# A four-block tower on one core: when the dense heads' pieces run in the last stage

## The chip, the cores and the metric

The kernel runs as one program on one core of a Trainium2 chip. Its time is the device time of one execution in microseconds; before the change the median of 3 runs is 13776.14 us (13771.75 to 13789.44).

## The reference, cut to what matters

The reference is a tower of four blocks over 4 sequences of 2048 tokens with 64 channels. The change touches only the last half block, a product-key memory attention with 8 heads:

```python
q = (x @ Wq).reshape(b, n, HEADS, DIM) * DIM ** (-0.5)
kv_scores, indices = _pk(x, Wq_pk, pk_keys)   # 16 of 64 x 64 keys, per token and head
ind = indices + offsets[None, None, :, None]
k = jnp.einsum('bnhk,bnhkd->bnhd', kv_scores, keys_table[ind])
v = jnp.einsum('bnhk,bnhkd->bnhd', kv_scores, values_table[ind])
sim = jnp.einsum('bihd,bjhd->bhij', q, k)
sim = jnp.where(causal, sim, neg)
attn = jax.nn.softmax(sim, axis=-1)
out = jnp.einsum('bhij,bjhd->bhid', attn, v)
return out.transpose(0, 2, 1, 3).reshape(b, n, HEADS * DIM) @ Wo
```

Each token and head picks 16 of 4096 table rows, mixes them with softmax weights into one key and one value, and then the head runs causal attention over its 2048 tokens.

## The kernel before, in words

The stage `mix_heads` works on 32 (sequence, head) pairs. 20 of them are "gathered" heads (kind `g`): GpSimd fetches the 16 rows of each token by indirect DMA (L2278), ScalarE scales them (`part_up`, L2479) and VectorE sums them (L2714). 12 are "dense" heads (kind `d`): no row is fetched; the whole table of the head lies in SBUF and is multiplied by a weight matrix that is made piece by piece. Each pair is cut into 4 quads of 512 tokens, a quad into 4 tiles of 128 tokens. So there are DQ = 48 dense quads, GQ = 80 gathered quads, and 512 tiles.

**A dense quad is 32 pieces** (one per 128 rows of the table's 4096), numbered k over all quads, 1536 in all. One piece is:
- `level` (TensorE, L2369): one bf16 matmul, 128x512, of the ranks into a PSUM bank, `DX` or the last bank of `S`;
- `lift` (ScalarE, L2521): a Relu of the bank into `V`;
- `cross` (TensorE, L2375 three times and L2376): four bf16 matmuls into the same bank;
- `grow` (ScalarE, L2525): Exp of the bank into `W`;
- `blend` (TensorE, L2385): an f32 matmul, `values` times `W`, summed up in `acc`.

After 32 pieces VectorE scales `acc` (`store`, L2743), and ScalarE copies it out when the quad's queries are made.

**The order is written out by hand, by sub-steps** s = 0 to 536. Every engine runs the same loop over s in its own in-order queue. In sub-step s, tile n = s - 24 is attended, the 16 picks of one tile of quad s // 4 are found on VectorE, 10 copies (COPIES) of gathered rows are scaled on ScalarE, and the pieces of `pieces(s)` are run. A tile at depth i in its sequence attends over i + 1 blocks of 128 keys, in chunks of four blocks: a quad g has 1, 2, 3 or 4 chunks by g % 4. Each chunk is a `flip` (TensorE transposes of the probabilities, L2343), a `take_flip` (ScalarE, L2517) and a `mixing` (TensorE, L2353).

In a sub-step TensorE and ScalarE interleave these in turns c = 0, 1, ...; there are as many turns as the most of chunks, pieces and extras (extras make q, k, v, ranks and the like, at most 4 of them):

```python
for c in range(turns(s)):
    if c < chunks(s):
        flip(n, c)
    if c < len(todo):
        cross(todo[c])
    if c < chunks(s):
        mixing(n, c)
    for use in extras(s)[c:c + 1]:
        extra(use)
    if c + 1 < len(todo):
        onward(todo[c + 1])
```

`onward(k)` is `blend(k - 1)` and `level(k)`. ScalarE does take_flip, grow, the extra, three copies of `part_up` and the next lift in each turn; the ten copies are out after the third turn and one more. `spare` and `second` choose the bank: pieces alternate between `DX` and the last bank of `S`, except beside tiles that need that bank of `S` (depth 12 and up in this or the next tile), where all go to `DX`.

A tile begins with `scores` (L2336), which waits for the Exp of the tile before (`attend`, ScalarE, L2508), as `S` is one buffer; `attend` waits for VectorE's `peak` (L2725). VectorE's `scale` (L2734) of tile n comes after `peak` of tile n + 1 and waits for the last `mixing` of tile n.

`first_piece(s)` (in the kernel before: 1536 pieces over 512 sub-steps, 3 in each from s = 9 to 520) decides which pieces a sub-step has. `pick_order` sorts the quads by a due sub-step so that picks come before gathers and pieces; `attend_order` is the fixed order in which quads are attended. SyncE reloads each quarter of `values` when its eight tiles are blended.

Of the kernel before, what the change touches and what calls it, by code (L numbers as in the profile page):

```python
# [4 lines left out]

# [1 line left out]

# [1958 lines left out]
HEADS, KEYS, TOPK, KV = 8, 64, 16, 2 * D  # L1968
# [4 lines left out]

PERIOD, BEFORE = 20, (0, 2, 4, 5, 8, 9, 10, 12, 14, 16, 18, 19)
LAG, UNITS_FROM, PIECES_FROM = 6, 12, 9
QUAD = 4
DQ, GQ = QUAD * len(D_HEADS), QUAD * len(G_HEADS)
QUADS = DQ + GQ
STEPS = QUAD * (QUADS + LAG) + 1
TILES = KEYS * KEYS // P  # L1980
COPIES = TOPK * GQ // QUADS
# [88 lines left out]
def gather_quad(g):  # L2070

    return *G_HEADS[g // QUAD], g % QUAD


def dense_quad(d):

    return *D_HEADS[d // QUAD], d % QUAD


def first_piece(s):  # L2080

    return TILES * DQ * (s - PIECES_FROM) // (QUAD * QUADS)


def pick_order():

    def due(kind, i):
        if kind == "g":
            return UNITS_FROM + QUAD * TOPK * i / COPIES - 6
        return PIECES_FROM + QUAD * QUADS * i / DQ - 9  # L2090

    return sorted([("g", i) for i in range(GQ)] + [("d", i) for i in range(DQ)], key=lambda x: (due(*x), x[0]))


def attend_order():

    order, d = [], 0
    for g in range(GQ):
        if g % PERIOD in BEFORE:
            order.append(("d", d))  # L2100
            d += 1
        order.append(("g", g))
    return order


def mix_heads(nc, table, h, hT, ident, ones, wsim, iota, wq, wo, mask, lanes, sel, counts, push, least):

    wsim_h = wsim[:].rearrange("d (p h k) -> d h p k", p=2, h=HEADS)
    picks, attends = pick_order(), attend_order()
    kinds = [attends[n // QUAD] for n in range(QUAD * QUADS)]  # L2110
    depth = [QUAD * (kinds[n][1] % QUAD) + n % QUAD for n in range(QUAD * QUADS)]
# [16 lines left out]
    def pieces(s):  # L2128

        return list(range(max(first_piece(s), 0), max(min(first_piece(s + 1), TILES * DQ), 0)))  # L2130
# [63 lines left out]
    with Scope(nc, "l3m") as u:  # L2194
# [91 lines left out]
        def _(pe):  # L2286
# [139 lines left out]
            for s in range(STEPS):  # L2426
                n, nxt = tile_at(s), tile_at(s + 1)
                todo = pieces(s)
                if todo:
                    onward(todo[0])  # L2430
                elif pieces(s - 1):
                    blend(TILES * DQ - 1)
                if nxt is not None:
                    scores(nxt, max((k + 1 for k in second if k < first_piece(s)), default=0))
                if n is not None:
                    pe.wait_ge(expd, n + 1)
# [11 lines that stand above are left out]
# [494 lines left out]
```

## Time and profile before

| what | us |
|---|---|
| median of 3 runs | 13776.14 |
| lowest and highest run | 13771.75, 13789.44 |
| span of the profiled execution | 17300.9 |
| of it, the stage of the change (from about 5850 on) | about 11450 |

The profiled execution's own time is its span, 17300.9 us; no unprofiled time is recorded for it, and it is 25.6% over the median of the runs. PE is TensorE's matmul, PEld its weight load, DVE VectorE, ACT ScalarE, POOL GpSimd, SP SyncE. In a row of a timeline the first number is the start in us from the span's start, the second the duration in us, and in square brackets stands the idle time of that engine just before and what ended it. "remote" and "another core or an unknown queue" stand where the profile cannot name what ended an idle time.

### The profile page before, as it was taken

The page shows a single profiled execution, that of the slowest core. Times are in us where ns is not written, and L with a number is a line of the kernel's source. Part 1 is how long each engine was busy: PE and PEld are TensorE (multiplying, and loading weights), DVE is VectorE, ACT ScalarE, POOL GpSimd, SP SyncE. Part 2 cuts the span into 40 slices and gives each one's busy share as a digit, 9 for nine tenths or more (in the row PEclk, how much of TensorE's full clock was granted, in tenths as well). Part 3 has the DMA queues.
Part 4 walks back from the last instruction along what each step waited for, and adds up shares of the span by engine and source line. Part 5 has one row for each costly group of instructions (what it writes and reads, how often), then busy time and mean ns, then how long its engine had stood idle before and what let it go on. Part 6 is the DMA issues. An engine that isn't in the chain of part 4 may idle for free.

```text
span 17300.9 us, 137100 instructions
## 1 busy us (share of the span) xinstructions
PE 10525.5 (61%) x38012; PEld 5367.1 (31%) x38012; DVE 9604.5 (56%) x22115; ACT 6663.5 (39%) x13997; POOL 6947.2 (40%) x5868
## 2 busy tenths in 40 slices
PE   1564555554655366666666666666666666666667
PEld 1341222222212123333333333333333333333334
DVE  3327888887675654555544555455554454555542
ACT  0113333341002144444444444444444444444443
POOL 2004666764000254444444444444444444444442
PEclk9556777776677577877787778787877777777776
DMA  0001222221000111111111111111111111111110
GB/s 20 0 13 69 90 105 102 107 89 69 12 11 5 31 40 38 35 41 35 40 34 38 37 38 38 35 38 37 38 35 41 33 41 34 38 38 37 38 35 20
DMA packets 538556, 722.95 MB, mean 42 GB/s; under 512 B 412866, under 2 KB 420593, under 8 KB 503386
## 3 DMA queue, kind: packets, MB, share of 16 engines
q0 software_dynamic: 168448, 338.54, 7.4%
q1 hardware_dynamic: 369418, 376.55, 7.1%
q8 instruction: 270, 4.42, 0.1%
q14 instruction: 420, 3.44, 0.1%
HBM read 697.87 MB, written 8.42 MB: 41 GB/s over the span
## 4 chain that ended last, share of the span: by engine, by line
PE 25%; another core or an unknown queue 16%; ACT 14%; issue 7%; DVE 3%; DVEq 1%; ACTq 0%
ACT l3m_spread L2479 5%; PE l3m_O L2353 5%; PE l3m_acc L2385 4%; PE l3m_DX L2375 4%; PE l3m_S L2336 3%; ACT l3m_V L2521 2%; PE l3m_T L2343 2%; ACT l3m_prob L2508 2%; PE l3m_S L2375 2%; ACT l3m_W L2525 2%; ACT l3m_probT L2517 1%; PE l3m_DX L2376 1%; PE l3m_T L2296 1%; PE l3m_T L2321 1%
## 5 line engine op out<-in xcount | busy, mean ns | idle before, releaser
L2278 POOL DMA_INDIRECT l3m_got<-in_l_table,l3m_row x5120 | 4995.9, 976 | 6236.5 <-ACT l3m_spread L2479 3620.8
L2385 PE MATMUL l3m_acc<-l3m_W,l3m_values 128*128 128x512 f32 x3072 | 2014.8, 743 | 922.9 <-issue 512.8
L2734 DVE SCALAR_TENSOR_TENSOR tower_h<-l3m_O,l3m_pinv,tower_h 128x64 f32<-128x64 f32 x512 | 145.4, 284 | 3520.3 <-PE l3m_O L2353 2621.6
L2479 ACT ACTIVATE l3m_spread<-l3m_got,l3m_weight 128x128 f32<-128x128 f32 x5120 | 1924.1, 493 | 12.4 <-issue 12.4
L2517 ACT ACTIVATE l3m_probT<-l3m_T 128x512 f32<-128x512 f32 (+3 forms) x1280 | 679.8, 531 | 1756.8 <-remote 1108.3
L2353 PE MATMUL l3m_O<-l3m_vo_g,l3m_probT 128*128 128x64 f32 x5440 | 861.0, 306 | 678.5 <-ACT l3m_probT L2517 459.5
L1262 POOL TENSOR_TENSOR m_mul<-m_st,m_wide_c 128x2048 f32<-128x2048 f32 x256 | 1157.5, 4521 | 149.9 <-DVE m_st L1415 143.7
L2353 PEld LDWEIGHTS l3m_O<-l3m_vo_g,l3m_probT 128*128 128x128 f32 x5440 | 832.3, 222 | 916.2 <-ACT l3m_probT L2517 570.5
L2525 ACT ACTIVATE l3m_W<-l3m_DX 128x512 f32<-128x512 f32 x971 | 579.3, 597 | 1258.9 <-PE l3m_DX L2376 563.2
L2343 PE MATMUL l3m_T<-tower_ident,l3m_prob 128*128 128x128 f32 x4352 | 844.9, 317 | 286.9 <-issue 160.2
L2385 PEld LDWEIGHTS l3m_acc<-l3m_W,l3m_values 128*128 128x128 f32 x3072 | 592.9, 223 | 1301.5 <-issue 684.5
L1295 PE MATMUL m_W<-m_mul,tower_ident 128*128 128x512 f32 (+1 forms) x1536 | 836.9, 666 | 207.4 <-POOL m_mul L1262 206.4
L2375 PE MATMUL l3m_DX<-l3m_high,l3k_sel 128*128 128x512 bf16 x971 | 433.2, 446 | 823.6 <-ACT l3m_V L2521 626.5
L2343 PEld LDWEIGHTS l3m_T<-tower_ident,l3m_prob 128*128 128x128 f32 x4352 | 598.7, 164 | 1052.8 <-issue 789.2
L2521 ACT ACTIVATE l3m_V<-l3m_DX,l3k_least 128x512 bf16<-128x512 f32 x971 | 652.5, 672 | 614.6 <-remote 428.7
L1308 PE MATMUL m_W<-m_split,l1a_sel 128*128 128x512 bf16 x1024 | 374.8, 456 | 762.9 <-DVE m_st L1415 751.1
L2353 PE MATMUL l3m_O<-l3m_vo_d,l3m_probT 128*128 128x64 f32 x3264 | 520.9, 307 | 390.4 <-ACT l3m_probT L2517 196.3
L2336 PE MATMUL l3m_S<-l3m_kvT_g,l3m_qT 64*128 64x512 f32 (+3 forms) x1600 | 563.4, 691 | 317.1 <-ACT l3m_prob L2508 194.4
L2714 DVE TENSOR_REDUCE l3m_kv<-l3m_spread 128x128 f32<-128x2048 f32 x320 | 727.3, 2273 | 10.8 <-ACT l3m_spread L2479 10.6
L2725 DVE TENSOR_REDUCE l3m_nmax<-l3m_S 128x1 f32<-128x128 f32 (+15 forms) x512 | 661.2, 1291 | 48.7 <-issue 10.6
L2525 ACT ACTIVATE l3m_W<-l3m_S 128x512 f32<-128x512 f32 x565 | 337.2, 597 | 899.8 <-remote 432.7
L2353 PEld LDWEIGHTS l3m_O<-l3m_vo_d,l3m_probT 128*128 128x128 f32 x3264 | 498.1, 223 | 541.9 <-ACT l3m_probT L2517 266.9
(689 smaller groups left out, 21609.8 us busy)
## 6 DMA issues: line engine op xcount, KB each, us to landing
m_wide_c<-l1a_c SPq DMA_DIRECT2D x256, 1024.0 KB, 4.6
l3m_got<-in_l_table,l3m_row POOLq DMA_INDIRECT x5120
l3m_values<-in_l_table SPq DMA_DIRECT2D x288, 256.0 KB
l0i_img<-in_l_x SPq DMA_DIRECT2D x4, 1024.0 KB, 7.9
l2r_x<-l2a_hT SPq DMA_DIRECT2D x8, 512.0 KB, 5.5
qp_inw<-in_q_inw SPq DMA_DIRECT2D x1, 2336.0 KB, 7.8
l_kept<-l0t_xt,l0t_row POOLq DMA_INDIRECT x128
l1a_c<-m_mul SPq DMA_DIRECT2D x16, 128.0 KB, 2.6
```

Source lines behind the costliest of these rows:

```text
L1262: pool.tensor_tensor(mul[:, k % 2], st[:, k % 2], wide_c[:, k % CRING], ALU.mult).then_inc(multiplied, 1)
L1295: last = pe.matmul(W[:, 1, lo:hi], ident[:], mul[:, k % 2, lo:hi], start=(k == 0), stop=(k == 2 * DS - 1))
L2278: pool.indirect_dma_start(got[:, unit % GOT, j, :], None, table, bass.IndirectOffsetOnAxis(ap=row[:, unit // QUAD % RING, unit % QUAD, j:j ...
L2336: last = pe.matmul(S[:, c * CH:hi], qT[k:k + D, slot, t * P:(t + 1) * P], kvT[kind][k:k + D, c * CH:hi], start=True, stop=True)
L2343: last = pe.transpose(T[:, (a % 4) * P:(a % 4 + 1) * P], prob[:, a * P:(a + 1) * P], ident[:])
L2353: last = pe.matmul(O[:, n % 2 * D:(n % 2 + 1) * D], probT[:, (chunk0[n] + c) % 2, (a % 4) * P:(a % 4 + 1) * P], vo[kind][:, a, :], start=( ...
L2375: pe.matmul(bank(k), sel[:, k % TILES, :], x[:, k // TILES % 2, :], start=(i == 0), stop=False)
L2385: pe.matmul(acc[:], values[:, tile, :], W[:], start=(tile == 0), stop=(tile == TILES - 1)).then_inc(blended, 1)
L2479: copy = act.activation(spread[:, unit % 2, :, j], got[:, unit % GOT, j, :], ACT.Copy, scale=weight[:, g % RING, t, j:j + 1])
L2517: act.activation(probT[:, k % 2, 0:to], T[:, 0:to], ACT.Copy).then_inc(t_taken, 1)
L2521: act.activation(V[:], S[:, 3 * CH:] if k in second else DX[:], ACT.Relu, bias=least[:], scale=-1.0).then_inc(lifted, 1)
L2525: act.activation(W[:], S[:, 3 * CH:] if k in second else DX[:], ACT.Exp).then_inc(grown, 1)
```

## The change

`first_piece` is no longer a constant rate. `piece_starts` gives every dense quad a window of sub-steps: it begins where that of the quad before ends and ends LEAD = 4 sub-steps before the quad's first tile is attended. Inside the window the 32 pieces are shared in proportion to a weight of each sub-step: 3.0 where no tile is attended, 4.0, 3.5, 2.5 and 1.5 beside tiles of 1, 2, 3 and 4 chunks. `pick_order` takes the dense quads' due sub-step from the new starts.

```diff
+PIECE_SHARE, LEAD = (3.0, 4.0, 3.5, 2.5, 1.5), 4
...
-def first_piece(s):
-
-    return TILES * DQ * (s - PIECES_FROM) // (QUAD * QUADS)
-
-
-def pick_order():
-
-    def due(kind, i):
-        if kind == "g":
-            return UNITS_FROM + QUAD * TOPK * i / COPIES - 6
-        return PIECES_FROM + QUAD * QUADS * i / DQ - 9
...
+def piece_starts():
+
+    order = attend_order()
+    ends = [QUAD * (LAG + n) - LEAD for n, (kind, g) in enumerate(order) if kind == "d"]
+    starts, begin = [], PIECES_FROM
+    for d, end in enumerate(ends):
+        shares = []
+        for s in range(begin, end):
+            n = s // QUAD - LAG
+            shares.append(PIECE_SHARE[order[n][1] % QUAD + 1 if n >= 0 else 0])
+        sums = [0.0, *itertools.accumulate(shares)]
+        starts += [TILES * d + int(TILES * x / sums[-1] + 0.5) for x in sums[:-1]]
+        begin = end
+    return starts + [TILES * DQ]
+
+
+PIECE_STARTS = piece_starts()
+
+
+def first_piece(s):
+
+    return PIECE_STARTS[min(max(s - PIECES_FROM, 0), len(PIECE_STARTS) - 1)]
+
+
+def pick_order():
+
+    def due(kind, i):
+        if kind == "g":
+            return UNITS_FROM + QUAD * TOPK * i / COPIES - 6
+        return next(s for s in range(STEPS) if first_piece(s + 1) > TILES * i) - 9.5
```

## Rows read from the trace of the kernel before

**Rows 1.** Busy us by stretch (PE, PEld, DVE, ACT, POOL), granted clock, DMA: the stage.
```profile
6150.00:17055.00 10905.00, 7190.62 (x28651) 3752.71 (x28652) 5454.66 (x17453) 5106.80 (x12081) 4850.64 (x4973) 0.79 0.15 37
```

**Rows 2.** Idle time before L2508, then who waited for L2479 (us, times).
```profile
  DVE l3m_nmax L2725: 71.0, 43
...
  POOL l3m_got L2278: 3620.8, 265
```

**Rows 3.** Timeline of ACT, a sub-step beside a one-chunk tile.
```profile
7229.07 0.60 ACT L2525 ACTIVATE l3m_W<-l3m_DX 128x512 f32<-128x512 f32 x1 [1.13 <-issue]
7229.56 1.09 ACT L2479 ACTIVATE l3m_spread<-l3m_got,l3m_weight 128x128 f32<-128x128 f32 x3
7230.46 0.66 ACT L2521 ACTIVATE l3m_V<-l3m_S,l3k_least 128x512 bf16<-128x512 f32 x1
7232.24 0.60 ACT L2525 ACTIVATE l3m_W<-l3m_S 128x512 f32<-128x512 f32 x1 [1.13 <-PE l3m_S L2376]
...
7234.92 0.47 ACT L2508 ACTIVATE l3m_prob<-l3m_S,l3m_nmax 128x256 f32<-128x256 f32 x1 [0.63 <-DVE l3m_nmax L2725]
```

**Rows 4.** Timeline of PE in the same sub-step.
```profile
7223.09 1.02 PE L2385 MATMUL l3m_acc<-l3m_W,l3m_values 128*128 128x512 f32 x2
7224.05 0.70 PE L2336 MATMUL l3m_S<-l3m_kvT_d,l3m_qT 64*128 64x256 f32 x2
...
7228.00 0.39 PE L2375 MATMUL l3m_DX<-l3m_high,l3k_sel 128*128 128x512 bf16 x1 [0.32 <-issue]
...
7229.72 1.12 PE L2385 MATMUL l3m_acc<-l3m_W,l3m_values 128*128 128x512 f32 x2 [0.47 <-ACT l3m_W L2525]
```

**Rows 5.** Timeline of ACT, two sub-steps beside four-chunk tiles.
```profile
8813.86 0.60 ACT L2525 ACTIVATE l3m_W<-l3m_DX 128x512 f32<-128x512 f32 x1 [0.64 <-PE l3m_DX L2376]
...
8816.48 0.59 ACT L2517 ACTIVATE l3m_probT<-l3m_T 128x512 f32<-128x512 f32 x1
8817.70 0.60 ACT L2525 ACTIVATE l3m_W<-l3m_DX 128x512 f32<-128x512 f32 x1 [0.64 <-PE l3m_DX L2376]
...
8818.77 0.38 ACT L2517 ACTIVATE l3m_probT<-l3m_T 128x256 f32<-128x256 f32 x1
...
8334.94 0.60 ACT L2525 ACTIVATE l3m_W<-l3m_DX 128x512 f32<-128x512 f32 x1 [0.64 <-PE l3m_DX L2376]
...
8338.67 0.59 ACT L2517 ACTIVATE l3m_probT<-l3m_T 128x512 f32<-128x512 f32 x1
8339.90 0.60 ACT L2525 ACTIVATE l3m_W<-l3m_DX 128x512 f32<-128x512 f32 x1 [0.64 <-PE l3m_DX L2376]
...
8341.18 0.60 ACT L2517 ACTIVATE l3m_probT<-l3m_T 128x512 f32<-128x512 f32 x1 [0.28 <-PE l3m_T L2343]
```

**Rows 6.** Timeline of ACT at the end, where no pieces are left.
```profile
17215.00 0.60 ACT L2517 ACTIVATE l3m_probT<-l3m_T 128x512 f32<-128x512 f32 x1 [4.91 <-PE l3m_T L2343]
17218.51 0.60 ACT L2517 ACTIVATE l3m_probT<-l3m_T 128x512 f32<-128x512 f32 x1 [2.91 <-PE l3m_T L2343]
...
17249.69 0.60 ACT L2517 ACTIVATE l3m_probT<-l3m_T 128x512 f32<-128x512 f32 x1 [1.64 <-PE l3m_T L2343]
17251.92 0.60 ACT L2517 ACTIVATE l3m_probT<-l3m_T 128x512 f32<-128x512 f32 x1 [1.64 <-PE l3m_T L2343]
```

**Rows 7.** Busy time by stretch, as Rows 1: the end, and a four-chunk sub-step.
```profile
17212.00:17226.00 14.00, 11.43 (x46) 8.31 (x42) 2.26 (x3) 2.27 (x4) 0.00 (x0) 0.50 0.00 1
17243.00:17254.00 11.00, 8.84 (x46) 5.43 (x46) 2.53 (x3) 1.83 (x4) 0.00 (x0) 0.81 0.00 0
...
8327.00:8341.00 14.00, 12.80 (x78) 8.68 (x78) 11.72 (x30) 9.51 (x23) 1.89 (x2) 1.00 0.19 42
```

**Rows 8.** Chain of waits, 7221 to 7236 us, by line.
```profile
by line: DVE l3m_hot L2655 10.1%; issue 8.7%; DVE l3m_hot L2652 8.2%; DVE l3m_hot L2648 8.2%; PE l3m_O L2353 7.5%; DVEq L2732 5.5%; ACT l3m_probT L2517 4.0%; DVE tower_h L2734 3.8%; DVE l3m_where L2612 3.3%; DVE l3m_where L2605 3.2%; DVE l3
```

**Rows 9.** Idle time before store, L2743, and before blend, L2385 (us, times).
```profile
  PE l3m_acc L2385: 257.9, 25
...
  ACT l3m_W L2525: 994.0, 706
```

More of the change, by code:

```diff
@@ L8 @@
+import itertools
 from contextlib import ExitStack
@@ L2077, in dense_quad @@
     return *D_HEADS[d // QUAD], d % QUAD
-def first_piece(s):
-    return TILES * DQ * (s - PIECES_FROM) // (QUAD * QUADS)
-def pick_order():
-    def due(kind, i):
-        if kind == "g":
-            return UNITS_FROM + QUAD * TOPK * i / COPIES - 6
-        return PIECES_FROM + QUAD * QUADS * i / DQ - 9
-    return sorted([("g", i) for i in range(GQ)] + [("d", i) for i in range(DQ)], key=lambda x: (due(*x), x[0]))
 def attend_order():
@@ L2103, in attend_order @@
     return order
+def piece_starts():
[19 more added lines that the diff above has]
+        return next(s for s in range(STEPS) if first_piece(s + 1) > TILES * i) - 9.5
+    return sorted([("g", i) for i in range(GQ)] + [("d", i) for i in range(DQ)], key=lambda x: (due(*x), x[0]))
 def mix_heads(nc, table, h, hT, ident, ones, wsim, iota, wq, wo, mask, lanes, sel, counts, push, least):
```

## The prediction

> **What bounds the kernel now.** I read the views in this order: busy time by stretch, for the stage; idle time and waiters of single lines, for which engine waits for which; timelines of sub-steps, for the price of a turn; the chain of waits through one light sub-step.
>
> In the stage no engine is near full: of 10905 us TensorE is busy 7190.62, VectorE 5454.66, ScalarE 5106.80, GpSimd 4850.64, at a granted clock of 0.79 [rows 1]. So the stage runs by waits. VectorE is not the usual one: of the 512 times that ScalarE came to `attend`, it waited for VectorE's maximum 43 times, 71.0 us in all. Nor is GpSimd: it stood 3620.8 us until ScalarE had freed a buffer [rows 2]. What is left is the ring between TensorE and ScalarE: cross, grow, lift, the next cross, with copies in ScalarE's queue between. In the light sub-step grow starts at 7229.07 and again at 7232.24, a turn of 3.17 us, in which ScalarE stood 1.13 us before grow [rows 3], and TensorE 0.32 before cross and 0.47 before blend [rows 4]. In a heavy sub-step a turn with a chunk and a piece lasts 3.84 us (8813.86 to 8817.70), or 4.96 where an extra lies in it (8334.94 to 8339.90) [rows 5]. So the same piece costs 3.17 us in a turn of its own, but shares a 3.84 us turn with a chunk that would need 2.23 alone [rows 6].
>
> **The change, part by part.** No matmul, copy or DMA is added. 1536 pieces, 1280 chunks and 5120 copies stay; they are dealt out anew. Working `first_piece` through all 537 sub-steps (0 with no tile, 1 to 4 chunks with 128 sub-steps each), the pieces go from 45, 384, 384, 363, 360 to 41, 488, 420, 360, 227. But the windows are 8, 12 or 16 sub-steps long, so the rate swings too: sub-steps have 1 to 6 pieces instead of 3, and 28 of those with three chunks get 5. Counting turns by kind, before to after:
> - chunk and piece together: 1107 to 911;
> - piece without chunk: 429 to 625, of which 217 are the fourth or later turn of a sub-step (none before), and 21 fewer come earlier;
> - chunk without piece: 173 to 369.
>
> So 196 turns in which a chunk and a piece cover each other are pulled apart into two.
>
> 1. *A fourth or later piece turn.* The measured turn of 3.17 us holds three copies (1.09 us) [rows 3]. The ten copies are nearly out by the fourth turn, so ScalarE no longer holds it up and TensorE does: cross starts at 7228.00, blend at 7229.72, 1.72 us later, and a blend takes 0.96 (7223.09 to 7224.05) [rows 4]. 2.7 us. Low end 2.3: ScalarE's own ring, grow to lift 0.5 (as 7229.07 to 7229.56 with no copies) and lift to grow 1.78 (7230.46 to 7232.24) [rows 3]. High end 4.2: the 2.7 with TensorE at its lower clock, by the ratio of a chunk turn's 3.51 to 2.23 us [rows 6]. I take 2.7, since the dense stretches run at 1.00 [rows 7]. 217 x 2.7 = +586 us.
> 2. *Earlier piece turns that vanish*: 21 x 3.17 = -67 us.
> 3. *A combined turn that loses its piece.* 3.84 us becomes a chunk turn of 2.29 (8816.48 to 8818.77): 1.55 saved. With extras 4.96 becomes 2.51 if the extra is covered elsewhere (8338.67 to 8341.18): 2.45 saved, the high end [rows 5]. Low end 1.0: the extra stays in the turn and its hand-over of the single `T` bank is no longer covered by a blend, 4.96 against 2.23, plus the extra's own 1.1 (4.96 less 3.84), plus 0.6 for its copy out of `T`. I take 1.6, near the clean pair. 196 x 1.6 = -314 us.
> 4. *VectorE.* In the light sub-step shown ScalarE stood 0.63 us for VectorE before `attend` [rows 3], and the chain through this sub-step runs mostly over VectorE's lines [rows 8]: there a little of an added piece is free. 69 one-chunk sub-steps get more than 3 pieces: 69 x 0.63 = -43 us. Against this, `store` now always stands at the head of a sub-step, 48 times instead of 16, where VectorE waits for the last blend: it stood 257.9 us in 25 such waits, 10 each [rows 9]. Most of that wait it would spend before `scale` anyway; I charge 32 x 1.3 = +42 us, ends 0 and 3 each. These two cancel.
> 5. *At nothing.* Quads of picks swap places 12 times; the tails of a dense quad are still ready 5 sub-steps before its pieces but for one (2 to 4 before), so `level` waits for none of them. The last piece moves from sub-step 520 to 523, all before tiles that run anyway. SyncE's reload of a quarter of `values` starts 24 pieces before it is needed, at least 4 sub-steps at the densest; before blend no DMA stands among the waits, only grow (994.0 us) and issue [rows 9]. GpSimd follows ScalarE's copies, whose rate is unchanged; it is idle over half the stage [rows 1].
>
> Sum: 586 - 67 - 314 + 0 = +205 us against the profiled execution's 17300.9. I take the prices from clean turns with no stall in them, so they hold for an unprofiled run as well, and I add them unscaled to the median: 13776 + 205, rounded down a little for free time in light sub-steps, is **13970 us**. The bounds: low 217 x 2.3 - 67 - 196 x 2.45 - 43 = -91; high 217 x 4.2 - 67 - 196 x 1.0 + 96 = +744, though all ends at once are unlikely.
>
> **Rivals.**
> - *VectorE sets the pace of the light sub-steps* (faster). Then TensorE has time to spare beside one and two chunks, which is where the weights send the pieces. For it: the chain [rows 8], and that the 3500 us by which the profiled execution is longer hide its waits. Against: 43 waits [rows 2]. If the first added piece is free in all 105 sub-steps with one or two chunks that have over 3 pieces: 205 - 105 x 2.7 = -79, 13700 us. It decides from about 75 free pieces on.
> - *Only TensorE's work counts* (no change). The matmuls are the same, in number and shape, and if the gaps only move about, the time stays at 13776 us. For it: TensorE has the most busy time of all [rows 1]; against: the 1.13 us and 0.47 us gaps in every piece turn. The Trainium skill ("Perfetto Trace Analysis", Identifying the Most-Contended Engine) has it that time goes by the engine with the highest occupancy, with a caveat for TensorE; by that rule this rival would be the forecast.
> - *Bare chunk turns let the clock fall* (slower still). At the end of the stage, with no pieces, the granted clock is 0.50 in one stretch and 0.81 in another, against 1.00 where chunks and pieces alternate [rows 7]; a chunk turn lasts 3.51 us (17215.00 to 17218.51) in the first and 2.23 in the second [rows 6]. If all 196 new chunk turns run at the lower of the two levels (1.2 GHz): 196 x 1.28 = +251, 14220 us. Against: one turn with a piece comes first in most of them. The Trainium skill ("TensorE: Matmul & The Clock Gate", HAM oscillation) says that idle gaps of TensorE throttle it again, which the 0.50 stretch agrees with.
>
> **How the numbers follow.** Forecast (+60 to +350): 0.45. Clock or heavier added turns: 0.20. No change: 0.10. VectorE's pace: 0.25. Within 0.2% (28 us) a measurement of this kernel can't tell a change. So faster 0.25, same 0.10, slower 0.65. The range leaves out the far end of both the faster and the slower cases: 13690 to 14300 us.
>
> **What the changed profile would show.** Fourth and later piece turns of 2.5 to 3 us beside one-chunk tiles, where only copies thin out; bare chunk turns of 2.2 to 2.5 us; sub-steps beside one chunk with 5 or 6 pieces near 20 us; ScalarE's wait for VectorE at `attend` still small. I am wrong if light sub-steps keep their length while heavy ones shrink: then ScalarE's waits at `attend` were real in the unprofiled run. I am also wrong if removed pieces save the 2.45 us end each.

## The result, and the profile after

The changed kernel takes 14151.85 us (median of 4 runs, 14136.75 to 14162.62) against 13782.79 for the kernel before in the same series of runs: a ratio of 1.0269 (95% interval 1.0254 to 1.0283), 369 us slower. The forecast was 13970, the range 13690 to 14300. Some of the runs below, and the profile ahead of the prediction, fell into series of runs in which the kernel before takes 17300 to 17640 us instead of 13780 (of the runs below these are the ones on two other chips; whether that is the reason isn't known), so every kernel is compared only with others of the same series, and two single executions far above all others of theirs (19283.62 us of the kernel before, 19112.85 of `oldwin`) are in no ratio. For the rows I profiled the kernel before once more (`again`) where it takes 13780.43 us.

The busy times and the clock line of the page, of `again`:

```profile
span 13778.7 us, 137100 instructions
PE 9495.6 (69%) x38012; PEld 4958.1 (36%) x38012; DVE 9604.7 (70%) x22115; ACT 6627.9 (48%) x13997; POOL 7029.1 (51%) x5868
PEclk9655677777775777589999999999999999999996
```

The same of the changed kernel:

```profile
span 14160.9 us, 136522 instructions
PE 9675.2 (68%) x37434; PEld 5071.9 (36%) x38012; DVE 9611.3 (68%) x22115; ACT 6622.8 (47%) x13997; POOL 7004.6 (49%) x5868
PEclk9655777777776776698999998999998999999997
```

VectorE, ScalarE and GpSimd are busy as long as before, within 25 us. TensorE alone is busy 180 us longer, though it has no matmul more (some records of this trace are missing, 37434 of 38012), and in the last stage its clock digit falls from 9 to 8 in a few slices. Some of the same matmuls ran slower.

**Where the time went.** The attended tiles' Exp (one row of `attend` each, 512 of them) gives the length of every sub-step, from its start to the start of the next. Sorted by the chunks of the tile, from `again` and from the changed kernel, us; the last column is what the terms of the prediction give for the class (late turns x 2.7, earlier piece turns x 3.17, lost pairs x 1.6):

```
chunks   before   after   measured   by the terms
1        1722     1886    +164       109 x 2.7 - 5 x 3.17            = +278
2        1803     1989    +186       48 x 2.7 - 12 x 3.17            = +92
3        1994     2028    +34        60 x 2.7 - 63 x 1.6             = +61
4        2169     2172    +3         -133 x 1.6                      = -213
```

And the mean length of one sub-step, by chunks and pieces:

```
chunks   before, 3 pieces   after: 1       2       3       4       5       6
1        13.45                     -       11.56   12.80   15.05   16.24   21.66
2        14.09                     -       13.57   15.41   15.17   19.12   -
3        15.64                     22.00   13.97   14.48   19.17   20.27   -
4        17.03                     16.85   16.98   17.43   -       -       -
```

The four-chunk sub-steps, from which the change takes 133 of 360 pieces, did not get shorter. That is the surprise of the result. It holds tile by tile too, where the same attended tile is compared in both kernels: the 45 that lose two pieces are 0.17 us shorter, the 43 that lose one are 0.29 longer. (Cells with one piece beside three chunks and four beside three rest on 4 sub-steps each.)

### The profile page after: what moved, and what is told of

Its sections match the earlier page's. It is cut to its first block, busy times and chain, and to the rows that moved or that the text cites. A ratio compares the mean times of both kernels' runs of the same rounds, so it can differ in the third digit from the quotient of the medians.

```text
span 14160.9 us, 136522 instructions
## 1 busy us (share of the span) xinstructions
PE 9675.2 (68%) x37434; PEld 5071.9 (36%) x38012; DVE 9611.3 (68%) x22115; ACT 6622.8 (47%) x13997; POOL 7004.6 (49%) x5868
## 4 chain that ended last, share of the span: by engine, by line
PE 31%; ACT 15%; DVE 6%; issue 4%; DVEq 2%; POOL 1%; ACTq 0%; another core or an unknown queue 0%; DMA 0%; POOLq 0%
PE l3m_O L2374 6%; ACT l3m_spread L2500 5%; PE l3m_S L2357 5%; PE l3m_acc L2406 4%; PE l3m_DX L2396 4%; PE l3m_S L2396 3%; PE l3m_T L2364 3%; ACT l3m_V L2542 2%; ACT l3m_W L2546 2%; ACT l3m_prob L2529 2%; PE l3m_DX L2397 1%; ACT l3m_probT L2538 1%; PE l3m_T L2342 1%; PE l3m_T L2324 1%; POOL l3m_got L2299 1%
## 5 line engine op out<-in xcount | busy, mean ns | idle before, releaser
L2299 POOL DMA_INDIRECT l3m_got<-in_l_table,l3m_row x5120 | 5053.5, 987 | 3032.1 <-issue 1522.0
L2406 PE MATMUL l3m_acc<-l3m_W,l3m_values 128*128 128x512 f32 x3072 | 1742.7, 650 | 305.5 <-ACT l3m_W L2546 286.7
L2374 PEld LDWEIGHTS l3m_O<-l3m_vo_g,l3m_probT 128*128 128x128 f32 x5440 | 779.4, 212 | 378.8 <-ACT l3m_probT L2538 327.3
L2546 ACT ACTIVATE l3m_W<-l3m_DX 128x512 f32<-128x512 f32 x905 | 540.4, 597 | 670.7 <-PE l3m_DX L2397 663.9
L2406 PEld LDWEIGHTS l3m_acc<-l3m_W,l3m_values 128*128 128x128 f32 x3072 | 531.6, 198 | 639.3 <-ACT l3m_W L2546 523.5
L2529 ACT ACTIVATE l3m_prob<-l3m_S,l3m_nmax 128x128 f32<-128x128 f32 (+15 forms) x512 | 591.2, 1155 | 177.8 <-DVE l3m_nmax L2746 177.7
L2542 ACT ACTIVATE l3m_V<-l3m_DX,l3k_least 128x512 bf16<-128x512 f32 x905 | 606.1, 670 | 83.8 <-remote 52.5
L1406 DVE TENSOR_TENSOR m_W<-m_dtx,m_W 128x1024 f32<-128x1024 f32 x512 | 618.4, 1208 | 22.0 <-PE m_W L1309 21.4
L2546 ACT ACTIVATE l3m_W<-l3m_S 128x512 f32<-128x512 f32 x631 | 376.8, 597 | 539.7 <-PE l3m_S L2397 527.1
L1416 DVE TENSOR_TENSOR_SCAN m_st<-m_dA,m_st,m_W 128x1024 f32<-128x1024 f32 x256 | 600.8, 2347 | 22.0 <-issue 2.7
```

The lines of the kernel that those rows point to most:

```text
L2299: pool.indirect_dma_start(got[:, unit % GOT, j, :], None, table, bass.IndirectOffsetOnAxis(ap=row[:, unit // QUAD % RING, unit % QUAD, j:j ...
L2374: last = pe.matmul(O[:, n % 2 * D:(n % 2 + 1) * D], probT[:, (chunk0[n] + c) % 2, (a % 4) * P:(a % 4 + 1) * P], vo[kind][:, a, :], start=( ...
L2406: pe.matmul(acc[:], values[:, tile, :], W[:], start=(tile == 0), stop=(tile == TILES - 1)).then_inc(blended, 1)
L2529: act.activation(prob[:, 0:to], S[:, 0:to], ACT.Exp, bias=nmax[:, n % 2:n % 2 + 1], accum_out=psum[:, n % 2:n % 2 + 1]).then_inc(expd, 1)
L2542: act.activation(V[:], S[:, 3 * CH:] if k in second else DX[:], ACT.Relu, bias=least[:], scale=-1.0).then_inc(lifted, 1)
L2546: act.activation(W[:], S[:, 3 * CH:] if k in second else DX[:], ACT.Exp).then_inc(grown, 1)
```

## The added turns, and the turns that were to shrink

A one-chunk sub-step with six pieces, timeline of ACT in the changed kernel; these rows answer to [rows 3]:

```profile
8831.87 0.60 ACT L2546 ACTIVATE l3m_W<-l3m_DX 128x512 f32<-128x512 f32 x1 [1.13 <-PE l3m_DX L2397]
8835.04 0.60 ACT L2546 ACTIVATE l3m_W<-l3m_S 128x512 f32<-128x512 f32 x1 [1.13 <-PE l3m_S L2397]
8835.54 0.50 ACT L2500 ACTIVATE l3m_spread<-l3m_got,l3m_weight 128x128 f32<-128x128 f32 x1
8835.84 0.67 ACT L2542 ACTIVATE l3m_V<-l3m_DX,l3k_least 128x512 bf16<-128x512 f32 x1
8837.72 0.60 ACT L2546 ACTIVATE l3m_W<-l3m_DX 128x512 f32<-128x512 f32 x1 [1.21 <-PE l3m_DX L2397]
8840.40 0.60 ACT L2546 ACTIVATE l3m_W<-l3m_S 128x512 f32<-128x512 f32 x1 [1.50 <-PE l3m_S L2397]
8843.07 0.60 ACT L2546 ACTIVATE l3m_W<-l3m_DX 128x512 f32<-128x512 f32 x1 [1.50 <-PE l3m_DX L2397]
```

and of PE, the blend in one of these turns:

```profile
8841.05 1.12 PE L2406 MATMUL l3m_acc<-l3m_W,l3m_values 128*128 128x512 f32 x2 [0.47 <-ACT l3m_W L2546]
```

From grow to grow: 3.17 us with three copies, then 2.68, 2.68 and 2.67. The price of a late piece turn was 2.7. ScalarE stands 1.21 to 1.50 us in each and TensorE only 0.47, while it waits for grow. So TensorE's own work and this one hand-over make the turn, as supposed.

Now a quad of tiles with four chunks. First `again`, 3 pieces in each of its sub-steps, then the changed kernel, 1 in each; busy time by stretch, the columns are those of [rows 1]:

```profile
8462.30:8532.30 70.00, 60.62 (x316) 36.12 (x316) 39.80 (x129) 49.65 (x111) 40.18 (x43) 0.95 0.23 56
```

The same quad in the changed kernel:

```profile
8561.70:8627.90 66.20, 51.37 (x241) 33.30 (x244) 51.06 (x137) 36.98 (x85) 42.11 (x41) 0.78 0.14 40
```

Eight pieces fewer save 3.8 us instead of 8 x 1.6 = 12.8. The granted clock falls from 0.95 to 0.78. ScalarE's rows in this stretch show what the bare chunk turns cost:

```profile
8578.32 0.60 ACT L2538 ACTIVATE l3m_probT<-l3m_T 128x512 f32<-128x512 f32 x1 [1.10 <-PE l3m_T L2364]
8580.57 0.62 ACT L2538 ACTIVATE l3m_probT<-l3m_T 128x512 f32<-128x512 f32 x1
8583.79 0.62 ACT L2538 ACTIVATE l3m_probT<-l3m_T 128x512 f32<-128x512 f32 x1
...
8589.40 1.86 ACT L2529 ACTIVATE l3m_prob<-l3m_S,l3m_nmax 128x1920 f32<-128x1920 f32 x1 [2.22 <-DVE l3m_nmax L2746]
...
8623.94 0.60 ACT L2538 ACTIVATE l3m_probT<-l3m_T 128x512 f32<-128x512 f32 x1 [1.44 <-PE l3m_T L2364]
8627.45 0.60 ACT L2538 ACTIVATE l3m_probT<-l3m_T 128x512 f32<-128x512 f32 x1 [2.51 <-PE l3m_T L2364]
```

8578.32 to 8580.57 is a bare turn of 2.25 us, the quick one of [rows 6]. 8623.94 to 8627.45 is one of 3.51 us, the slow one, here in the midst of the stage. And at 8589.40 ScalarE waits 2.22 us for VectorE. In the 45 four-chunk sub-steps with one piece the mean clock was 0.80, and TensorE was busy 12.64 us in each; in those of `again` with three pieces it was 0.98 and 14.53 us. At the same speed two pieces fewer, an estimated 2.1 us each by [rows 4] (five bf16 matmuls of about 0.22 and a blend of 0.96), would leave 10.3 us. So by this estimate about 2.3 us of each came back as slower matmuls, and 0.7 us as a longer wait for VectorE (0.84 against 0.17 before the `attend` that ends the sub-step).

Over the stage as a whole ScalarE does not wait longer for VectorE than before. Idle time of ScalarE before `attend`, in `again`:

```profile
  DVE l3m_nmax L2725: 201.5, 124
```

In the changed kernel:

```profile
  DVE l3m_nmax L2746: 177.7, 75
```

Without the stalls of the first profile the wait is nearly three times the 71.0 us of [rows 2], but it does not grow by the change.

## The experiments

**The kernel before, profiled again.** `again`, no edit.

> The kernel before, profiled once more, to have a trace of it whose span is near its time. Turn theory (chunks and pieces cover each other in combined turns, and 196 of them were pulled apart): the same prices as in the changed kernel, piece turns of 3.17 us, combined turns of 3.2 to 5, bare chunk turns of 2.2 to 2.5. VectorE theory (light sub-steps last as long as VectorE needs): ScalarE's wait for VectorE at attend is several times the 71.0 us of the first trace. Time 13770 to 13800 us under both.

Measured: 13780.43 us, rows above. Both theories had something: the turns have the foretold prices, and the wait at `attend` is 201.5 us, 2.8 times that of the first trace.

**Only the windows.** `flatwin` is the changed kernel with

```diff
-PIECE_SHARE, LEAD = (3.0, 4.0, 3.5, 2.5, 1.5), 4
+PIECE_SHARE, LEAD = (1.0, 1.0, 1.0, 1.0, 1.0), 4
```

> The changed kernel with all five weights equal: only the windows of 8, 12 or 16 sub-steps are left, so 2, 3 or 4 pieces in a sub-step. Turn theory: combined turns 1107 to 1089 only, 108 late piece turns come and 90 earlier ones go: 108 x 2.7 - 90 x 3.17 - 18 x 1.6 = -22 us, so within 40 us of the kernel before. Swing theory (dense stretches with 4 pieces in each sub-step are what costs, or store at the head of a sub-step): 100 to 250 us slower than before.

Measured: 13929.28 us, ratio 1.0106 (1.0090 to 1.0123), +143 against 13786.47. A miss of the turn theory, which counts turns at one price wherever they lie; the swing theory's 100 to 250 us held. The trace has four-chunk sub-steps of 16.36, 17.27 and 20.09 us with 2, 3 and 4 pieces: a fourth costs three times what the third one's removal gives. Tile by tile against `again` the gap is wider: 3.00 us more with the fourth piece, 0.38 less without the third. So the swing of the rate by itself costs about 40% of what the change costs.

**Only the weights.** `oldwin` keeps the weights and cuts windows of 10 or 11 sub-steps:

```diff
-    ends = [QUAD * (LAG + n) - LEAD for n, (kind, g) in enumerate(order) if kind == "d"]
+    ends = [PIECES_FROM - (-TILES * (d + 1) // 3) for d in range(DQ)]
```

> The changed kernel with its weights, but with windows of 10 or 11 sub-steps, as the constant rate has them. Combined turns 1107 to 973, 134 fewer. Turn theory: the measured +369 us for 196 pulled apart is 1.9 us each, so 134 x 1.9 = +250 us (+143 by the prices of the prediction). Swing theory: the windows were the cost, less than +100 us is left.

Measured: 14103.16 us, ratio 1.0228 (1.0207 to 1.0248), +317. The weights alone cost most of the 369, more than the 250 foretold by the turn theory, and the swing theory's bound of 100 is refuted. The two parts overlap (143 + 317 is more than 369): both push sub-steps away from three pieces; that some pushes cancel where both act is my reading, not shown.

**The reverse.** `reverse` is the kernel before with 2, 3, 3 and 4 pieces beside 1, 2, 3 and 4 chunks:

```diff
+PIECE_SHARE = (3, 2, 3, 3, 4)
...
+        starts.append(min(starts[-1] + PIECE_SHARE[beside] + (s == PIECES_FROM), TILES * DQ))
```

> The kernel before with 2, 3, 3 and 4 pieces beside tiles of 1, 2, 3 and 4 chunks (3 where there is no tile, 4 in the first sub-step): the reverse of the change. Combined turns 1107 to 1234. Turn theory: 127 piece turns of 3.17 us go and 127 bare chunk turns grow by 1.6 to 1.9: 160 to 200 us faster than before, about 13600 us. VectorE theory: one-chunk sub-steps can't get shorter, four-chunk ones get longer: 50 to 200 us slower than before.

Measured: 14014.11 us, ratio 1.0171 (1.0154 to 1.0188), 228 us slower. This is the clearest miss of the turn theory: 127 more pairs, and slower. By class of sub-step, against `again`: 1722 to 1557 us beside one chunk, 2169 to 2536 beside four. So one-chunk sub-steps could get shorter, against the VectorE theory, but the removed piece turn gave 1.3 us on the mean and not 3.17. That mean is of two kinds of quad. Busy time by stretch for a quad of one-chunk tiles, first in `again`:

```profile
8716.20:8770.90 54.70, 41.94 (x154) 18.47 (x155) 48.16 (x153) 33.87 (x88) 38.54 (x36) 0.94 0.18 46
```

The same quad in `reverse`:

```profile
8817.20:8871.20 54.00, 35.39 (x122) 16.45 (x121) 48.12 (x151) 29.46 (x82) 38.58 (x36) 0.84 0.17 43
```

VectorE is busy 48 of 54 us in both: here it does set the pace, and the clock falls to 0.84 on top. Another quad of one-chunk tiles, in `again`:

```profile
7380.10:7432.10 52.00, 39.61 (x150) 16.64 (x150) 32.68 (x114) 33.07 (x90) 39.50 (x42) 0.99 0.20 53
```

and in `reverse`:

```profile
7434.50:7473.70 39.20, 31.70 (x122) 14.47 (x122) 32.97 (x120) 28.41 (x81) 29.75 (x32) 0.96 0.20 52
```

Here VectorE has only 33 us of work, and four pieces fewer give 12.8 us, 3.2 each, the price of the prediction. Of the 32 one-chunk quads 15 end sub-steps in a wait for VectorE in `reverse`, and gain 0.3 us a sub-step; 17 do not, and gain 2.1. In all, ScalarE waits 320.8 us for VectorE before `attend`, against 201.5. The fourth pair beside four chunks is in the timeline of ACT in `reverse`:

```profile
8583.44 0.60 ACT L2539 ACTIVATE l3m_W<-l3m_DX 128x512 f32<-128x512 f32 x1 [0.64 <-PE l3m_DX L2390]
...
8587.89 0.60 ACT L2539 ACTIVATE l3m_W<-l3m_DX 128x512 f32<-128x512 f32 x1 [0.64 <-PE l3m_DX L2390]
...
8591.03 0.69 ACT L2535 ACTIVATE l3m_V<-l3m_DX,l3k_least 128x512 bf16<-128x512 f32 x1 [0.49 <-PE l3m_DX L2383]
...
8592.85 0.60 ACT L2539 ACTIVATE l3m_W<-l3m_DX 128x512 f32<-128x512 f32 x1 [0.75 <-PE l3m_DX L2390]
```

Turns of 4.45 and 4.96 us, where all pieces use the one bank `DX`, so that level, lift and cross follow each other (0.49 us of idle before lift). The sub-steps went from 17.03 to 20.09 us: 3.06 for a piece, which is most of why the reverse loses.

**The pick order.** `oldpick` is the changed kernel with the old due sub-steps; `flatpick` is `flatwin` with them:

```diff
-        return next(s for s in range(STEPS) if first_piece(s + 1) > TILES * i) - 9.5
+        return PIECES_FROM + QUAD * QUADS * i / DQ - 9
```

> The changed kernel with the pick order of the kernel before: only the pieces are dealt out anew. The change moved 32 of the 60 sub-steps with dense picks beside one-chunk tiles to four-chunk tiles (28 to 60), where VectorE's maximum is long too. Pick theory (VectorE is loaded at the wrong places): 60 us or more of the 369 go, ScalarE's wait at attend falls below the 177 us of the changed kernel. Turn and clock theory: the time stays within 30 us of the changed kernel.

> The changed kernel with equal weights and the pick order of before: only the windows of 8, 12 and 16 sub-steps are left. Equal weights with the new picks measured 146 us over the kernel before. Convex-cost theory (a four-chunk sub-step costs 3.1 us for a fourth piece and gives back 0.3 to 0.7 for a third one taken away: 44 x 3.06 - 35 x 0.67 = +111): 110 to 150 us over before, as with the new picks. Pick theory: under 80 us over before.

Measured, where the kernel before takes 17583.56 us: 17831.00 (ratio 1.0124, 1.0092 to 1.0156) and 17684.86 (1.0057, 1.0039 to 1.0075). Neither says much alone, as the changed kernel had not been timed in that series. So four kernels were run together next. First the control, the changed kernel itself:

> The changed kernel once more, beside the other three on one chip, since the last four runs fell on a chip where the kernel before takes 17580 us. Every theory: 2.5 to 2.9% over the kernel before where that takes 13780 us; less where it takes 17580, as the stalls there come on top of both.

Measured: 17857.47 against 17637.10, ratio 1.0125 (1.0094 to 1.0155), 220 us slower. So the change costs less here; that the stalls, which both kernels have, cover a part of the cost is the likely reason and was not tested.

> The changed kernel with the pick order of before, again. Pick theory: over 60 us faster than the changed kernel on the same chip. Turn and clock theory: within 30 us of it.

Measured: 17864.47, 7 us from the control, with ranges that overlap. So the pick order did nothing that shows in this series; where the kernel before takes 13780 us it was not tried. Whether `flatpick` differs from `flatwin` can't be told: 1.0057 and 1.0106 are from different series. Its 101 us over the kernel before lie between the two theories' figures.

**More matmuls to keep the clock.** `warm` and `warm2` are one kernel, the changed one with

```diff
+                    elif todo and c < chunks(s):
+                        pe.wait_ge(grown, todo[-1] + 1 if todo else TILES * DQ)
+                        for i in range(3):
+                            pe.matmul(DX[:], push[:], sel[:, 4 * i:4 * i + 4, :].rearrange("p t j -> p (t j)"),
+                                      start=True, stop=True)
```

between cross and mixing of TensorE's loop.

> The changed kernel with three added bf16 matmuls of 128x512, whose result nobody reads, between flip and mixing of each bare chunk turn in a sub-step that has pieces (325 turns). Clock theory (TensorE's granted clock is 0.80 and 0.87 in four-chunk sub-steps with 1 and 2 pieces against 0.98 with 3, so the pieces taken away save nothing): the clock of these sub-steps rises to over 0.95, they shorten by 1 to 2 us each, 90 to 180 us in all. Work theory: 325 x 0.65 us of matmuls come on top, 0 to 200 us slower.

> The changed kernel with three unread matmuls in each of the 325 bare chunk turns beside pieces, again. Clock theory: 90 to 180 us faster than the changed kernel on the same chip. Work theory: as fast, or up to 200 us slower.

Measured: `warm` 17728.34 against 17583.56 (1.0081, 1.0056 to 1.0105), 103 us by the medians under `oldpick` of the same series, which stands for the changed kernel as far as the pick order does nothing; `warm2` 17779.23 (17755.64 to 17811.93) beside the control's 17857.47 (17850.95 to 17859.56): 78 us faster with 975 matmuls more. The ranges do not overlap, so the work theory's "as fast or slower" is out. By class against the control, 82 us came out of the four-chunk sub-steps (3099 to 3017), the others changed by 16 or less. With one piece they have a clock of 0.81 instead of 0.66 and last 22.54 instead of 23.71 us, though TensorE has more matmuls in them; with two pieces it is 0.77 instead of 0.73, and 25.31 instead of 26.03 us. The gain of `warm2` is under the 90 to 180 foretold, and the clock did not reach 0.95; probably three matmuls don't fill the idle time where stalls come on top.

**The same at the end of the kernel before.** `warmtail` and `warmtail2` put these matmuls into the kernel before, in the 15 last sub-steps alone, which have no pieces at all:

```diff
+                    elif not todo and s > PIECES_FROM and not pieces(s - 1) and c < chunks(s):
```

> The kernel before, with the same three matmuls in the 15 last sub-steps alone, which have no pieces and a granted clock of 0.53 to 0.59. Clock theory: these sub-steps go from 14.5 and 17.9 us to some 12 and 14.5, 35 to 55 us faster than the kernel before in all, so under 13750 us. Work theory: 50 x 0.65 us, 0 to 30 us slower.

> The kernel before with unread matmuls in the 15 last sub-steps, again. Clock theory: the 52 us that it gained at 17580 us come back at 13780, some 13730 us, as its last sub-steps lasted 17.9 and 14.5 us there and should now last 12.1 and 11.0: 7 x 5.8 + 7 x 3.5 = 65. Work theory: no gain.

Measured: 17531.90 against 17583.56 (0.9970, 0.9956 to 0.9984), and 17562.06 against 17637.10 (0.9950, 0.9933 to 0.9967): 52 and 75 us faster than the kernel before, as the clock theory foretold (52 against 35 to 55, 75 against 65), and both intervals leave no change out. Busy time by stretch for a quad of four-chunk tiles without pieces, 4 sub-steps, in the kernel before (the profile ahead of the prediction):

```profile
17150.80:17226.00 75.20, 60.79 (x220) 42.08 (x220) 10.98 (x16) 17.68 (x28) 0.00 (x0) 0.52 0.00 1
```

and in `warmtail2`:

```profile
17466.10:17516.80 50.70, 44.07 (x265) 28.07 (x268) 10.98 (x16) 17.61 (x29) 0.00 (x0) 1.00 0.00 1
```

48 matmuls more (the profile misses 3 of their records, so 265 rows instead of 220), and 24.5 us less. The clock went from 0.52, the lower of its two levels (1.2 GHz) all but throughout, to 1.00. The Trainium skill ("TensorE: Matmul & The Clock Gate", HAM oscillation) says that idle gaps, in its case waits for a DMA between groups of matmuls, put TensorE back to half its clock. This pair of rows agrees so far that the clock came back when the gaps of copy and hand-over were filled. But these gaps are short: in the slow quad TensorE is busy 60.79 of 75.20 us, and none of its waits is over 1.05 us. The kernel with these matmuls beats the kernel before and the changed one; in a series where the kernel before takes 13780 us it was not run. In `again` this quad took 75.5 us too, so the gain should be alike.

## Why the prediction was right, and where it was not

Direction and range held; the size was 1.9 times the forecast (369 against 194). It lay outside the band of the forecast case (+60 to +350, chance 0.45), in that of the rivals with slower clock or heavier turns (0.20), which is why the range was wide enough. The terms missed the classes of one to four chunks by -114, +94, -27 and +216 us, so a part of the misses cancelled in the sum; that much of the hit is luck.

1. *A late piece turn, 2.7 us.* Measured 2.68, and the 12 one-chunk sub-steps with six pieces pay 8.2 us for three of them. But for the fourth piece one-chunk sub-steps went up by 1.6 us only (13.45 to 15.05), as 0.53 us of waiting for VectorE and 0.33 before `scores` went away. That was step 4's free time, and it was worth more than the 0.63 taken there: +164 for the class instead of +278.
2. *Earlier piece turns that vanish, 3.17 us.* In `reverse` one gave 1.3 us on the mean: 2.1, and up to 3.5, in the quads without a wait for VectorE, 0.3 in those with one. With 21 of them here it matters little.
3. *A combined turn that loses its piece, 1.6 us.* This is the step that failed. Beside three chunks it holds (tile by tile 1.61 us less with one piece less). Beside four it is 0.0 to 0.1 a piece: -213 foretold, +3 measured. The rival "bare chunk turns let the clock fall" is what took its place; it was priced at +251 for all 196 turns. `warm2` shows a part of it by intervention, 78 us in its series. The 2.3 us by busy time in each of 45 sub-steps (and 13.83 against 12.4, 1.4 us, in 43 with two pieces) make about 165 us, which is an estimate and not tested. Of the other 51 of the 216, 36 are the longer wait for VectorE in those sub-steps (45 x 0.67 + 43 x 0.14), and 13 are the 32 four-chunk sub-steps that kept three pieces and last 17.43 us instead of 17.03.
4. *VectorE and `store`.* The two were set against each other at 0. VectorE stood 340.8 us before all `store`s instead of 262.6, but ScalarE's wait for it at `attend` fell by 24 us, and at the `attend` behind a sub-step with `store` from 80.5 to 62.4. So the traces show no sign that the longer wait reached the ring; it was not tested by itself.
5. *At nothing: picks.* Held in the series where it was tried: 7 us of difference.

Of the rivals, "VectorE sets the pace" is true with two pieces, in about half of the one-chunk quads of `reverse`; "only TensorE's work counts" is excluded, as five kernels with the same matmuls took 13780 to 14152 us.

**What stays open.** Two-chunk sub-steps with an unchanged three pieces last 15.41 us instead of 14.09 in the changed kernel, and 15.57 in `flatwin`, but 14.11 in `oldwin`. That is 106 us that no count of turns explains, and tile by tile 86 of them remain. It goes with the windows and not with the weights; the clock there is 0.92 against 0.97. `store` is not the bulk of it: 12 of the 80 sub-steps hold one and last 15.77 us, the other 68 still 15.34, against 13.93 for those without `store` in `again`. Whether it is the bank order, the neighbours or the dense picks and extras that now lie beside them was not tried.

## What to carry to other kernels

When work is dealt out over slots of an interleaved loop, look at the length of a slot as a function of what is in it, on both sides of the present share: beside four-chunk tiles it is nearly flat below three pieces, where the clock falls, and steep above (3.0 us for a fourth), and beside one-chunk tiles it is flat below three only where VectorE is full. All four uneven deals tried here lost, the plausible one and its reverse. A price read off a turn (2.68, 3.17 us) was paid in full only where nothing else filled or had left a gap, and taking work away was where it misled most. And where TensorE runs through copies and hand-overs with nothing between, unread matmuls in the gap can be worth more than they cost: 52 to 78 us here.

## What the runs showed of the hardware

The same kernel took 13780 us in some series of runs and 17300 to 17640 in others, where the profile shows stalls whose end it cannot name: before the copies of L2517 ScalarE stood 1108.3 us in 210 waits marked "remote" in the first profile, and in none in `again`. A cost of 369 us in a series of the first kind was 220 in one of the second. TensorE's granted clock was 0.52 over a stretch in which it was busy 81% of the time with no gap over 1.05 us, and 48 added matmuls of 128x512 brought it to 1.00 and shortened the stretch of 75.2 us by 24.5.
